# Ranged semaphore clears, and a new division of the expert attention's routing, choice and last unit

## The reference

```python
ss = sigmoid(x @ Ws).reshape(b, t, H, E); sd = sigmoid(x @ Wd).reshape(b, t, H, E)
ms = _topk_mask(ss, 3); md = _topk_mask(sd, 3)
q = einsum('bthed,bthe->bhtd', q5, sd * md)      # q5 = x @ Wq
k, v = (einsum('bthed,bthe->bhtd', a, ss * ms) for a in (k5, v5))
out = softmax(q * scale @ k.T) @ v               # per head
o5 = einsum('bthd,dm->bthm', out, Wo)
return einsum('bthem,bthe->btm', o5, md)
```

## Time and profile before

| | us |
|---|---|
| median of 3 runs (lowest to highest) | 2741.61 (2740.38 to 2743.81) |
| the profiled execution's own time | 2743.55 |
| its span in the profile | 2741.8 |
| first expert attention, from the end of the attention's last L2095 to its own last clear | 1361.4 to 1986.7 |
| second expert attention, from the end of its barrier to its last clear | 2114.2 to 2736.0 |
| busy: PE / DVE / ACT / POOL | 2399.0 / 1981.8 / 1503.8 / 1837.6 |

### The profile page before, as it was taken

How to read it: one execution, slowest core, us unless ns; L and a number is a source line. 1 busy time by engine, 2 the same in 40 slices (tenths; PEclk the granted TensorE clock), 3 DMA queues, 4 the chain that set the end, 5 groups by cost and what they waited for, 6 DMA issues and landing times. The chain is left out here.

```text
span 2741.8 us, 56038 instructions
## 1 busy us (share of the span) xinstructions
PE 2399.0 (87%) x21310; PEld 1556.0 (57%) x21310; DVE 1981.8 (72%) x3620; ACT 1503.8 (55%) x2069; POOL 1837.6 (67%) x1732
## 2 busy tenths in 40 slices
PE   6887787886899999999789999998788799999986
PEld 3555544644566676666556666665534466666655
DVE  7998545446677777777488888886286888888862
ACT  4222122322788888888625665556452256665564
POOL 1888100000999999999637899999610388999985
PEclk9899788988899999999889999999888999999998
DMA  1000000002689998899615555555411055555554
GB/s 44 1 1 0 0 23 13 1 23 64 123 159 161 151 157 162 150 153 163 118 49 90 96 93 95 95 95 97 76 31 53 20 99 94 93 93 93 95 102 80
DMA packets 763819, 226.74 MB, mean 83 GB/s; under 512 B 745992, under 2 KB 754696, under 8 KB 763552
## 3 DMA queue, kind: packets, MB, share of 16 engines
q1 hardware_dynamic: 763552, 223.16, 44.8%
HBM read 20.70 MB, written 1.05 MB: 8 GB/s over the span
## 5 line engine op out<-in xcount | busy, mean ns | idle before, releaser
L2275 PE MATMUL banks<-g_w,normed_t 128*128 128x320 f32 x1536 | 512.2, 460 | 42.2 <-DVE g_scratch L2580 38.3
L1575 POOL TENSOR_TENSOR g_p_lo<-g_p,g_p_hi 128x512 bf16<-128x512 f32 (+1 forms) x256 | 416.0, 1645 | 43.3 <-POOL g_z L2469 21.6
L1764 DVE TENSOR_REDUCE at_negmax<-banks 128x1 f32<-128x1024 f32 x256 | 301.5, 1219 | 154.6 <-PE banks L1676 154.6
L2275 PEld LDWEIGHTS banks<-g_w,normed_t 128*128 128x128 f32 x1536 | 265.7, 192 | 224.0 <-issue 81.0
L1741 POOL TENSOR_TENSOR at_p_lo<-at_p,at_p_hi 128x640 bf16<-128x640 f32 x256 | 356.0, 1407 | 13.2 <-ACT at_p_hi L1729 11.4
L1588 DVE TENSOR_REDUCE g_negmax<-banks 128x1 f32<-128x1024 f32 x256 | 310.3, 1217 | 32.8 <-PE banks L1499 30.4
L1565 ACT CAST g_r_hi<-banks 128x512 bf16<-128x512 f32 x128 | 74.9, 585 | 427.7 <-PE banks L1510 427.7
L1552 ACT ACTIVATE g_p<-banks,g_negmax 128x1024 f32<-128x1024 f32 x256 | 285.1, 1114 | 9.6 <-DVE g_negmax L1588 8.3
L1722 ACT ACTIVATE at_p<-banks,at_negmax 128x1024 f32<-128x1024 f32 x256 | 285.4, 1115 | 6.3 <-DVE at_negmax L1764 6.3
L1676 PE MATMUL banks<-at_k_t,at_q 64*128 64x512 f32 x1024 | 258.0, 623 | 18.5 <-POOL at_k_t L2025 9.7
L1499 PE MATMUL banks<-g_k_t,g_q 64*128 64x512 f32 x1024 | 254.4, 615 | 12.3 <-ACT g_p L1552 6.3
(11 more groups left out here) (414 smaller groups left out, 6327.3 us busy)
## 6 DMA issues: line engine op xcount, KB each, us to landing
at_swapped<-at_crossed SPq DMA_DIRECT2D x128, 128.0 KB, 2.8
g_w<-in_ex_w SPq DMA_DIRECT2D x2, 2880.0 KB, 11.5
f_w<-in_W SPq DMA_DIRECT2D x2, 1024.0 KB, 5.6
at_rope<-in_rope SPq DMA_DIRECT2D x1, 2048.0 KB, 9.8
at_t_hi<-at_p_hi SPq DMA_TRANSPOSE x128, 3.6
at_t_lo<-at_p_lo SPq DMA_TRANSPOSE x128, 3.6
g_t_hi<-g_p_hi SPq DMA_TRANSPOSE x128, 4.0
g_t_lo<-g_p_lo SPq DMA_TRANSPOSE x128, 3.8
```

Of the source, the lines that this page charges most:

```text
L1575: self.nc.gpsimd.tensor_tensor(self.part(self.p_lo, j, h), self.p[:, j % 2, h, 0:self.WIDTH[h]], self.part(self.p_hi, j, h), ALU.subtract) ...
L1764: self.nc.vector.tensor_reduce(self.negmax[:, j % 2, h:h + 1], self.core.banks[:, first:first + 2, :], AX.XY, ALU.max, negate=True).then_i ...
L2275: nc.tensor.matmul(out[:, 0:ED], core.xt[:, at:at + P], w[:, kind * H + tile // (T * BATCH) * 2 + h, :], start=True, stop=True).then_inc(p ...
```

## The change

Four things, with no change to what is computed.

1. `Core.clear` sorts the semaphores' numbers and clears each run of consecutive numbers by one instruction.
2. Routing: `dve_normalise` and GpSimd's L2462 become `dve_route`. VectorE forms share = mask x reciprocal (128x10, both inputs in SBUF) and multiplies the attention result in PSUM by it into `routed` (128x640, two buffers). GpSimd only adds to z. The reciprocal stays.
3. Choice: the first half of pair 0 is chosen as before. All other comparisons are made by VectorE ahead: pair 0's second half and pair 1 before the first product, pairs 2 and 3 before the first maxima; each is four instructions (by distance d between experts, in bf16). GpSimd counts (eight instructions a pair) and multiplies the gates by the mask; VectorE in between makes the mask (`limit`). Pairs 0 and 1 are counted in the lead-in, pairs 2 and 3 one instruction a step for j < 18.
4. Last unit: orders of instructions on TensorE, ScalarE and VectorE.

```diff
     def clear(self):
-        for handle in self.in_use:
-            self.nc.gpsimd.sem_clear(handle)
+        numbers = sorted(handle.num for handle in self.in_use)
+        for first, last in self.runs(numbers):
+            self.nc.gpsimd.sem_clear(range(first, last + 1))
...
-    def dve_normalise(self, dve, j):
+    def dve_route(self, dve, j, kept, added):
...
         dve.wait_ge(self.recip_ready, j + 1)
-        self.nc.vector.tensor_tensor(self.o[...], o[:, :, 0:64], self.core.col(self.recip[:], 64), ALU.mult).then_inc(self.o_ready, 1)
+        self.nc.vector.tensor_tensor(self.share[:], kept, self.core.col(self.recip[:], 5), ALU.mult).then_inc(self.share_ready, 1)
+        dve.wait_ge(self.share_ready, j + 1)
+        if j >= 2:
+            dve.wait_ge(added, j - 1)
+        self.nc.vector.tensor_tensor(self.routed[:, j % 2], o[:, :, 0:64].unsqueeze(2).to_broadcast([P, 2, 5, 64]),
+                                     self.share[:].unsqueeze(3).to_broadcast([P, 2, 5, 64]), ALU.mult).then_inc(self.o_ready, 1)
... # PE, last unit: project_out of the step before after turn_out; project_out of this step behind both halves of values
-                if unit + 1 == UNITS and t > 2:
-                    project_out(*done_in(t - 1)[1])
                 beside(0)
                 hs.transpose(pe, j)
                 for k, tile in finishing[0:1]:
                     turn_out(k, tile)
+                if unit + 1 == UNITS and t > 2:
+                    project_out(*done_in(t - 1)[1])
...
                 hs.subtract(pe, j)
-                for k, tile in finishing[0:1]:
-                    project_out(k, tile)
...
-                for k, tile in finishing[1:2]:
-                    turn_out(k, tile)
                 if j:
                     hs.values(pe, j - 1, 1)
                 beside(2)
+                for k, tile in finishing[0:1]:
+                    project_out(k, tile)
+                for k, tile in finishing[1:2]:
+                    turn_out(k, tile)
... # ACT, last unit
                 hs.act_copy(act, j)
+                for k, tile in finishing[0:1]:
+                    place_out(k)
                 if not last:
                     hs.act_exp(act, j + 1, 0)
-                for k, tile in finishing[0:1]:
-                    place_out(k)
... # GpSimd
-                step(g.tensor_tensor(routed[:], hs.o[...] ..., mask[...] ..., ALU.mult))
+            for tile in range(T):
+                sum_queries(tile)
+            for pair in range(2):
+                for k in range(8):
+                    count_duels(pair, k)
+            for pair in range(2):
+                keep(pair)
+            for tile in range(T, LEAD - 1):
                 sum_queries(tile)
             for j in range(STEPS):
                 for h in range(2):
                     hs.pool_lo(pool, j, h)
+                if j < 18 and j % 9 < 8:
+                    count_duels(2 + j // 9, j % 9)
+                elif j < 18:
+                    keep(2 + j // 9)
... # VectorE, lead-in and steps
-            choose((0,), range(T))
+            choose_first()
+            dve.wait_ge(gates_ready, CHUNKS)
+            compare(0)
+            compare(1)
...
-            choose((0,), range(T, 2 * T))
+            compare(2)
+            compare(3)
...
+                if tile in (4, 6):
+                    limit(tile // 2 - 2)
...
                     hs.dve_split_values(dve, 0)
-                    choose((1,), range(2 * T))
... # last unit: the add of a tile two places later than its projection's old place
-                for k, tile in finishing[0:1]:
-                    add_out(k, tile)
+                if unit + 1 == UNITS and t > 2:
+                    add_out(*done_in(t - 1)[1])
...
-                    hs.dve_normalise(dve, j - 1)
+                    route(j - 1)
...
-                if j < 30:
-                    choose_part(2 + j // 15, j % 15)
+                if j in (7, 16):
+                    limit(2 + j // 9)
```

More of the change, by code:

```diff
@@ L82, in clear, with runs @@
     def clear(self):
-        for handle in self.in_use:
-            self.nc.gpsimd.sem_clear(handle)
+        numbers = sorted(handle.num for handle in self.in_use)
+        for first, last in self.runs(numbers):
+            self.nc.gpsimd.sem_clear(range(first, last + 1))
         self.in_use = []
         self.nc.all_engine_barrier()
+    def runs(self, numbers):
+        starts = [n for n in numbers if n - 1 not in numbers]
+        return [(a, next(n for n in numbers if n >= a and n + 1 not in numbers)) for a in starts]
     def row(self, ap, tiles=TILES):
@@ L2163, in expert_attention_stage @@
         mask = sb("mask", [P, PAIRS, 2, 2 * TILES, E])
-        beats = [sb(f"beats{e}", [P, 2 * 2 * TILES, E - 1 - e]) for e in range(E - 1)]
-        lost = sb("lost", [P, 2 * 2 * TILES, E - 1])
+        beats = [sb(f"beats{e}", [P, 2 * 2 * T, E - 1 - e]) for e in range(E - 1)]
+        lost = sb("lost", [P, 2 * 2 * T, E - 1])
+        ahead = sb("ahead", [P, PAIRS, 2, 2 * TILES, E * (E - 1) // 2], BF16)
         scratch = sb("scratch", [P, 6 * 2 * ED])
@@ L2459, in route @@
                 pool.wait_ge(hs.o_ready, j + 1)
-                if t == 0 and unit in (0, 1, 2, 4, 6):
-                    pool.wait_ge(mask_ready, (0, 1, 2, 4, 6).index(unit) + 1)
-                step(g.tensor_tensor(routed[:], hs.o[:, unit % BATCH, t].unsqueeze(2).to_broadcast([P, 2, E, D]),
-                                     mask[:, unit // BATCH, 1, 2 * tile:2 * tile + 2, :].unsqueeze(3).to_broadcast([P, 2, E, D]), ALU.mult))
-                one, two = (routed[:, h].rearrange("p e c -> p (e c)") for h in range(2))
+                one, two = (hs.routed[:, j % 2, h].rearrange("p e c -> p (e c)") for h in range(2))
                 if unit < BATCH:
@@ L2528, in limit, with choose_first @@
-            def limit(pairs, tiles):
-                count = part(mask, pairs, tiles)
-                step(v.tensor_scalar(count, count, float(TOP), None, ALU.is_lt))
-                dve.sem_inc(mask_ready, 1)
-            def keep(pairs, tiles):
-                own = part(gate, pairs, tiles)
-                step(v.tensor_tensor(own, own, part(mask, pairs, tiles), ALU.mult))
-            def choose(pairs, tiles):
+            def choose_first():
+                own, count, behind = (t[:, 0, :, 0:2 * T] for t in (gate, mask, lost.rearrange("p (z w n) e -> p z w n e", z=1, w=2)))
+                beat = [b.rearrange("p (w n) e -> p w n e", w=2) for b in beats]
@@ L2539, in choose @@
                 for e in range(E - 1):
[L2540 removed]
+                    step.later(v.tensor_tensor(beat[e], own[:, :, :, e:e + 1].to_broadcast([P, 2, 2 * T, E - 1 - e]), own[:, :, :, e + 1:E],
+                                               ALU.is_ge))
                 step.wait()
                 for e in range(E - 1):
[L2543 removed]
+                    step.later(v.tensor_reduce(behind[:, :, :, e], beat[e], AX.X, ALU.add))
@@ new lines, in choose_first, with compare @@
+                step(v.tensor_tensor(count[:, :, :, 0:E - 1], count[:, :, :, 0:E - 1], behind, ALU.subtract))
+                step(v.tensor_scalar(count, count, float(TOP), None, ALU.is_lt))
+                step(v.tensor_tensor(own, own, count, ALU.mult))
+            def compare(pair):
+                own, beat = gate[:, pair, :, rows_left(pair)], ahead[:, pair, :, rows_left(pair)]
+                for d in range(1, E):
+                    ins = v.tensor_tensor(beat[:, :, :, duels(d)], own[:, :, :, 0:E - d], own[:, :, :, d:E], ALU.is_ge)
+                ins.then_inc(compared, 1)
@@ L2567, in apply_gates, with limit @@
+            def limit(pair):
+                dve.wait_ge(counted, pair + 1)
+                count = mask[:, pair, :, rows_left(pair)]
+                v.tensor_scalar(count, count, float(TOP), None, ALU.is_lt).then_inc(limited, 1)
             def apply_gates(n, bank):
@@ L2594, in sum_keys, with route @@
                 v.tensor_reduce(tok[:, 1, t], k_product[:, tile % 2], AX.X, ALU.add).then_inc(k_ready, 1)
+            def route(j):
+                unit, t = j // T, j % T
+                row = 2 * (unit % BATCH * T + t)
+                hs.dve_route(dve, j, mask[:, unit // BATCH, 1, row:row + 2, :], z_ready)
             def add_out(k, tile):
```

77 lines of the change are left out of this document (30 added, 47 removed).

## The result

The changed kernel takes 2661.12 us (median of 4 runs, 2658.89 to 2663.67) against 2742.71 (2740.38 to 2744.23) for the kernel before beside it: a ratio of 0.9704, with a 95% interval of 0.9687 to 0.972. That is 81.6 us less, where 64 were forecast; the time lies in the range, at its lower end. The profiled executions stand at 2743.55 and 2659.56, 84.0 apart.

The account below looks back on a forecast made before the run. No one engine bounds the whole: barriers wait on clears, lead-ins on VectorE, units 2 to 6 on GpSimd, the last unit on instruction order. Terms 23.0 + 7.7 + 18.2 + 11.7 + 3.0 = 63.6 less gave 2678 us, range 2660 to 2702.

Parts of the forecast that it names:

- clears: Eight barriers between stages: 311 single semaphore clears less at 74 ns, all on the path, 23.0 us less.
- lead-in: Start of both expert stages: choice for pair 1 leaves, less added comparisons and limits; 4.3 and 3.4, together 7.7 us less.
- units 0 and 1: First units of the expert stages: the choice's parts leave, the route comes, no change.
- units 2 to 6: Expert stages: pace passes from GpSimd to TensorE with about 0.1 a step lost; 9.1 us less a stage, 18.2 in both.
- last unit: Last unit of both expert stages: new orders bring steps to TensorE's own 7.2 us; 6.7 and 5.0, together 11.7 less.
- tail: End of both expert stages: cheaper product on VectorE and earlier last low halves; 1.5 us less a stage, 3 in both.
- Rival C: At the barriers, a range clear costs by its numbers; 23 us less gain, 2701; chance 0.1.
- rival A: Units 2 to 6: the share is held up in most steps, costing 9 to 17 us; 2687 to 2695; chance 0.22.
- rival D: Steps with projections: share falls behind a 2.14 us low half, slower than before; 2790 if in half; chance 0.03.
- the rule: VectorE instructions with two SBUF inputs and GpSimd's take turns on a shared port pair, locked for a whole instruction.
- rival B: Last unit: the transposing transfers pace it, so the 11.7 us gain goes; 2690; chance 0.12.
- the larger gains: Whole kernel: 2663 us if no step loses its 0.1 and the last unit gives 14; the rest of the chances.

Follow-up runs that it names:

- lead_delay: Changed kernel with four unused repeats of the values' split on VectorE where the choice for pair 1 had stood; 2677.79 us, ratio 0.9773.
- route_only: Kernel before with only the routing moved to VectorE, the choice staying wholly on VectorE; 2741.6 us, ratio 1.000.
- last_only: Kernel before with only the last unit's new orders of instructions; 2730.88 us, ratio 0.996.
- after_again: The changed kernel itself, unchanged, timed again in the rounds of later experiments; 2663.71 us, ratio 0.9715.
- clears_only: Kernel before with only the semaphore clears made by ranges; 2717.03 us, ratio 0.9913.
- values_pool: Changed kernel with the low half of the values' split given to GpSimd, g_v held once; 2680.26 us, ratio 0.9765.
- values_two: Changed kernel with the values' low half on GpSimd behind the queries' sums and g_v held twice; 2647.8 us, ratio 0.9657.

## Why the prediction was right, and where it was short

The mechanisms were right and the place of the time in the range was partly luck. 2661.12 is 1.1 us inside the lower end of 2660 to 2702, and the prediction had given only 0.03 to gains larger than its forecast's. Of the profiled 84.0, by step (both stages):

| step | forecast | measured |
|---|---|---|
| clears | −23.0 | −21.6 |
| lead-in | −7.7 | −15.0 |
| units 0 and 1 | 0 | −3.2 |
| units 2 to 6 | −18.2 | −20.8 |
| last unit | −11.7 | −15.4 |
| tail | −3.0 | −3.8 |
| other stages | 0 | −4.3 |

**Clears.** Right in place and nearly in size: 17 rows where "some 18" were expected, and the next work 0.7 to 1.1 after the last. Rival C is half true: a range clear does cost by its numbers, 304 ns for 49, 244 for 39 and 178 for 26, thus 5.5 ns a number (304 − 178 over 23). The 17 clears sum to 2.4 us where 17 of 44 ns would be 0.7: 1.6 more, about the 1.4 by which the forecast missed.

**Lead-in: the term most mis-sized.** The step said: 5.5 leaves, 0.6 to 1.5 comes back for comparisons, 0.6 for limits. The 5.5 was right, and so was the 1.0 for the first eight comparisons: where the first projection starts at the same time (15.0 and 14.8 us into the second stage), the first product starts at 16.4 before and at 17.4 after. What was charged for the rest was not paid. The maxima start 2.1 us behind the start of the first scores before and 2.0 after, so the last eight comparisons (3.62 us, 0.5 forecast) cost nothing; from these scores to the values' split are 18.4 us in both, so the limits (0.23 + 0.32, 0.6 forecast) cost nothing either.

And the prediction asked only what VectorE does in this stretch. Of the twelve matmuls behind TensorE's idle 6.86 us in the second stage, eight took 0.74 us or more (the first 0.90) and the last three 0.43, which is what they take now (0.54 where one starts behind a wait): the lower of TensorE's two clock levels, 1.2 instead of 2.4 GHz. That is 2.1 us in this stage (5.74 − 3.60) and 1.7 in the first (5.33 − 3.60), which left with the choice and came back with lead_delay. In the second stage the sum is 5.5 + 2.1 + 0.1 for the stretch behind the split, less 1.2 ahead of it: 6.5, as measured. In the first it is 7.3 + 1.1 = 8.4, and that this stage gains 1.1 ahead of the split, where the second loses 1.2, is luck. The first projection stood at 16.0 us there before, behind a low granted clock (0.50 in the stage's first 16 us), and at 14.7 after; but it stands at 14.8 to 15.0 in route_only and last_only, which keep the old choice, and at 16.0 again in after_again. So some 13 of the 15.0 are the change's.

**Steps.** Right in mechanism: GpSimd had paced units 2 to 6 and TensorE does now; the share at 0.20 us speaks against rival A, and a low half holds it up, as rival D wanted, only in the last unit (six of the 128 shares, 0.88 us at most). Two sizes were off. Steps take 7.77 and 8.51 flat, so the 0.1 that the forecast lost in each was not lost. Unit 1 had been called TensorE's pace at 66.4, but the choice's parts had cost there: with the choice shared it is 64.9. Units 3 to 5 take 65.4, as their first step is longer (9.5). What the prediction did not say is how much its parts lean on one another. The route alone gives nothing, the choice alone nothing in units 2 to 6; they had been summed as if each stood in the other's presence, which the change happened to grant.

The hold-up of the earlier trace rows is seen in the few places where it falls. The `limit` of step 7, 0.32 in the lead-in, and GpSimd beside it:

```profile
2190.65 1.04 DVE L2574 TENSOR_SCALAR g_mask<-g_mask 128x320 f32<-128x320 f32 x1
```

```profile
2190.35 3.33 POOL L1581 TENSOR_TENSOR g_p_lo<-g_p,g_p_hi 128x512 bf16<-128x512 f32 x2 [0.24 <-POOL g_z L2478]
```

The first of these two low halves ends at 2191.50, the limit at 2191.69. It has one input in SBUF, not two, so the rule as the prediction put it doesn't speak of it; what holds it up is not tested. And the last share, 0.17 at its best:

```profile
2632.02 3.24 POOL L1581 TENSOR_TENSOR g_p_lo<-g_p,g_p_hi 128x512 bf16<-128x512 f32 x2 [0.24 <-POOL g_z L2481]
```

```profile
2634.41 0.88 DVE L1603 TENSOR_TENSOR g_share<-g_mask,g_recip 128x10 f32<-128x10 f32 x1
```

It ends at 2635.29, 0.03 behind the low halves, at a place worth 0.7 us. Twenty of the 128 shares take more than 0.25 us, and each of them ends 0.02 to 0.03 behind a GpSimd instruction. The share has two inputs in SBUF, and the rule that the prediction took from the Trainium skill ("SBUF — State Buffer", section "SBUF: two separate sides") agrees with this.

**Last unit.** Right in mechanism (rival B out: 48.5, not 56), short by 3.7: three of the seven intervals are 6.88 and the mean is 6.9, where 7.2 was estimated from TensorE's rows, and TensorE is busy for 45.6 of the 48.5 us (46.8 of 57.0 before). That the overlap of its pieces at their edges makes the difference to 7.2 is argued, not shown. The route has its part: with it on GpSimd the seven intervals are 50.0 (last_only), the figure forecast, and without it 48.5; the three steps of 6.88 are the same in both, and the 1.5 lie in the unit's first three intervals and its last.

**Tail.** Near in the sum alone: 1.5 was forecast for each stage, and 3.5 and 0.3 are measured. In both the last low halves end 1.4 us sooner and the product takes 0.82 instead of 1.26, as forecast. But counted from the last once-a-step weight load the last route starts at 8.5 instead of 11.5 us in the first stage, with a granted clock of 1.00 up to it instead of 0.78, and at 11.7 instead of 11.5 in the second, at 0.85 in both. In after_again the first stage's gain is 2.0. What sets that start is open.

**Slips in the prediction's own working.** The 329 clears include the loading stage's one, so the eight barriers have 328. In the earlier trace rows the comparison count of 128x256 takes 0.41 us at its shortest elsewhere in the trace and 1.06 there, so it was held up for 0.65, not 0.8. TensorE's terms for the last unit add up to 7.4, not 7.2, which would have made the forecast 8.9 instead of 11.7. Units 2 to 6 have 60 steps without turning in both stages, not 56. And the larger gains come to 2670 by the bounds given for them, not to 2663. None of these touches a mechanism; with the third put right the forecast would have been further from the 15.4 measured.

**Other stages.** Not forecast. The linear attention is 1.5 shorter in clears_only and in after_again alike, 3.6 in the changed kernel's first profile; the softmax attention varies from 693.8 to 697.8 over these runs. How much of the 4.3 the change makes stays open, as does why the linear attention's 1.5 goes with the clears.

## What to carry to other kernels

An edit that fills an engine and one that empties it have to be priced together: here the one is worth 0 and the other 16 alone, and 40 both. Where an engine's wait is removed, look at the clock of TensorE behind the wait as well as at the wait; and where work moves to another engine, ask which buffer it reads and who writes that next (values_pool lost 16 to 19 us to it, values_two gained 13 with a second buffer).

## What the runs showed of the hardware

One clear over a range of semaphores took 44 ns for the shortest ranges and 5.5 ns more for each number, where one by one they came 71 to 77 ns apart. Behind 6.9 us of idleness twelve 128x320 matmuls took 5.17 and 5.74 us rather than 3.60. The same 128x1040 subtraction took 1.23 us at its shortest on VectorE and 2.16 on GpSimd. Twenty of 128 products of 128x10, with both inputs in SBUF, took 0.30 to 0.88 us instead of 0.17, and each ended 0.02 to 0.03 behind a GpSimd instruction.
